# A decoder of four layers on one core: half of each layer norm's normalising moves from ScalarE to GpSimd, and the order tables are laid anew

## The reference

```python
def _layernorm(x, axis=-1, eps=1e-05):
    m = jnp.mean(x, axis=axis, keepdims=True)
    v = jnp.var(x, axis=axis, keepdims=True)
    return (x - m) / jnp.sqrt(v + eps)
```

## Time and profile before

| | us |
|---|---|
| median of 3 runs | 5380.19 |
| lowest and highest | 5375.60, 5387.07 |
| span of the profiled execution | 5378.0 |
| PE busy | 4667.4 (87%) |
| DVE busy | 3288.8 (61%) |
| ACT busy | 2478.0 (46%) |
| POOL busy | 779.1 (14%) |

### The profile page before, as it was taken

The page is one execution under the profiler, slowest core; times in us unless marked ns, Lnnn a source line. Parts: engine busy times, 40 slices in busy tenths (PEclk is TensorE's granted clock), DMA queues, the critical chain, the costliest instruction groups (busy, mean ns, idle before and its releaser), DMA issues.

```text
span 5378.0 us, 128488 instructions
## 1 busy us (share of the span) xinstructions
PE 4667.4 (87%) x54601; PEld 3416.4 (64%) x54601; DVE 3288.8 (61%) x8433; ACT 2478.0 (46%) x5054; POOL 779.1 (14%) x841
## 2 busy tenths in 40 slices
PE   5668878899898989889898989889898989898877
PEld 4346656677676767666676767666676767666554
DVE  6754677555657475656657575656757575756542
ACT  3325545435444454444545454444545454544331
POOL 5550100101011110101011110101011111101000
PEclk7678989999899999999999999999999999999997
DMA  1132100012110101111010101111010101010000
GB/s 63 28 98 64 33 2 2 4 52 61 33 32 11 58 17 47 28 39 36 15 51 11 54 20 47 28 39 36 21 44 11 54 20 50 24 35 25 11 22 28
DMA packets 154184, 181.62 MB, mean 34 GB/s; under 512 B 62890, under 2 KB 82450, under 8 KB 152850
## 3 DMA queue, kind: packets, MB, share of 16 engines
q1 hardware_dynamic: 153618, 173.41, 10.8%
HBM read 162.50 MB, written 10.55 MB: 32 GB/s over the span
## 4 chain that ended last, share of the span: by engine, by line
PE 64%; DVE 16%; ACT 7%; issue 5%; POOL 1%; DMA 0%; SPq 0%; POOLq 0%; DVEq 0%; ACTq 0%
PE g_pair L2759 8%; PE g_pair L2774 8%; PE g_pair L1626 6%; DVE g_tops L1703 6%; PE g_pair L1599 6%; PE g_pair L1649 5%; ACT g_keys_exps L1679 4%; PE g_pair L1996 2%; PE g_pair L1986 2%; PE g_pair L1433 1%; PE g_pair L1611 1%; PE g_pair L1660 1%; PE g_pair L2060 1%; PE g_pair L2360 1%; PE g_pair L1569 1%
## 5 line engine op out<-in xcount | busy, mean ns | idle before, releaser
L1679 ACT ACTIVATE g_keys_exps<-g_pair 128x1024 f32<-128x1024 f32 (+1 forms) x768 | 745.8, 1018 | 646.9 <-PE g_pair L1626 645.8
L1703 DVE TENSOR_REDUCE g_tops<-g_pair 128x8 f32<-128x1024 f32 (+1 forms) x768 | 748.7, 1006 | 329.8 <-PE g_pair L1599 328.1
L1412 POOL TENSOR_TENSOR g_rstd<-g_rstd,minus_half 128x4 f32<-128x4 f32 x224 | 231.2, 1033 | 3578.1 <-DVE g_rstd L1394 3573.5
L2774 PEld LDWEIGHTS g_pair<-region,g_keys_exps 128*128 128x128 f32 x4096 | 514.1, 192 | 142.6 <-issue 133.0
L2759 PE MATMUL g_pair<-g_xT,region 128*128 128x512 f32 x1024 | 551.9, 621 | 9.6 <-DVE g_keys_exps L2799 4.4
L2774 PE MATMUL g_pair<-region,g_keys_exps 128*128 128x128 f32 x4096 | 546.1, 278 | 4.5 <-DVE g_base L2806 3.9
L1626 PE MATMUL g_pair<-g_qa,g_keys_exps 32*77 32x128 f32 (+1 forms) x12288 | 463.5, 290 | 72.8 <-DVE g_o L1724 46.5
L1649 PE MATMUL g_pair<-g_keys_exps,g_v 77*32 77x128 f32 (+1 forms) x12288 | 444.9, 289 | 83.7 <-DVE g_tops L1703 74.7
L1626 PEld LDWEIGHTS g_pair<-g_qa,g_keys_exps 32*77 32x77 f32 (+1 forms) x12288 | 397.8, 175 | 171.7 <-DVE g_o L1724 78.8
L1599 PE MATMUL g_pair<-g_keys_exps,g_qa 32*128 32x256 f32 (+1 forms) x6144 | 392.5, 371 | 101.5 <-ACT g_keys_exps L1679 84.1
L1649 PEld LDWEIGHTS g_pair<-g_keys_exps,g_v 77*32 77x32 f32 (+1 forms) x12288 | 333.7, 115 | 200.3 <-DVE g_tops L1703 140.0
(11 more groups left out here) (379 smaller groups left out, 8541.9 us busy)
## 6 DMA issues: line engine op xcount, KB each, us to landing
region<-L_w_in SPq DMA_DIRECT2D x512, 256.0 KB, 2.9
region<-xT_in SPq DMA_DIRECT2D x16, 256.0 KB, 2.8
z_scratch<-m_z SPq DMA_DIRECT2D x4, 1024.0 KB, 5.4
g_qa<-xT_in SPq DMA_DIRECT2D x16, 256.0 KB, 2.9
g_oT_sc<-z_scratch SPq DMA_DIRECT2D x64, 64.0 KB, 2.6
g_o<-x_in SPq DMA_DIRECT2D x16, 256.0 KB, 3.1
out<-g_x SPq DMA_DIRECT2D x16, 256.0 KB, 2.3
setup_weights<-prepared_in SPq DMA_DIRECT2D x1, 2589.5 KB, 10.7
```

The source lines that it names most:

```text
L1412: e.tensor_tensor(g.rstd[:, :], g.rstd[:, :], g.s["minus_half"], ALU.pow).then_inc(*b.gpsimd(st + " rstd"))
L1679: e.activation(g.p[0:nk, 2 * k:2 * k + 2, :, :].rearrange("p g u q -> p (g u q)"), b.pair[st][k][0:nk, :, :].rearrange("p r c -> p (r c)") ...
L1703: e.tensor_reduce(top_columns(g, k), src, AX, ALU.max).then_inc(*b.vector(f"{st} top {n} {k}"))
L2774: ins = e.matmul(bank[1][:, n * D:(n + 1) * D], g.gated_hid[:, x % 2, c, n * T:(n + 1) * T], weights.part(f"w2 {x}", c), start=c == n == 0 ...
```

## The change

ACT's two operations of each norm go (`normalize_scalar` is deleted, 448 operations over the kernel). `normalize_gpsimd` takes them over, behind its power, in the form DVE uses: (x - mean) x rstd with two per-partition scalars, as a TENSOR_SCALAR on POOL, each waiting for the power's result. Since that form needs no shift, DVE's shift operation goes too (224). All who waited for ACT's "normal 2" or "normal 3" now wait for POOL's. `ORDER` of all five engines and `GIVEN` are laid anew; the opening's tables stay as they are. The steps of a batch number 291 on PE as before, 190 on ACT (218 before), 474 on DVE (488) and 61 on POOL (33).

```diff
     yield from between
-    e.wait_ge(*b.gpsimd[st + " rstd"])
-    e.scalar_tensor_tensor(out=g.shift[:, :], in0=g.mean_var[:, :, 0], scalar=-1.0, in1=g.rstd[:, :],
-                           op0=ALU.mult, op1=ALU.mult).then_inc(*b.vector(st + " shift"))
-    yield
     for n in range(2):
         e.wait_ge(*b.gpsimd[st + " rstd"])
         e.tensor_scalar(out[:, n, :], src[:, n, :], g.mean_var[:, n, 0:1], g.rstd[:, n:n + 1],
...
-def normalize_gpsimd(e, b, st):
+def normalize_gpsimd(e, b, st, src, out):
 
     g = b.g
     e.wait_ge(*b.vector[st + " variance"])
     e.tensor_tensor(g.rstd[:, :], g.rstd[:, :], g.s["minus_half"], ALU.pow).then_inc(*b.gpsimd(st + " rstd"))
     yield
-
-
-def normalize_scalar(e, b, st, src, out):
-
-    g = b.g
-    e.wait_ge(*b.vector[st + " shift"])
     for n in range(2, SEQS):
-        e.activation(out[:, n, :], src[:, n, :], ACT.Identity, bias=g.shift[:, n:n + 1], scale=g.rstd[:, n:n + 1]
-                     ).then_inc(*b.scalar(f"{st} normal {n}"))
+        e.wait_ge(*b.gpsimd[st + " rstd"])
+        e.tensor_scalar(out[:, n, :], src[:, n, :], g.mean_var[:, n, 0:1], g.rstd[:, n:n + 1],
+                        ALU.subtract, ALU.mult).then_inc(*b.gpsimd(f"{st} normal {n}"))
         yield
...
-            e.wait_ge(*b.scalar[f"{st} normal {n}"])
+            e.wait_ge(*b.gpsimd[f"{st} normal {n}"])
...
-    yield from normalize_scalar(e, b, st, g.x, g.x)
     e.wait_ge(*b.tensor[st + " turned"])
...
-    e.wait_ge(*b.scalar["end normal 3"])
+    e.wait_ge(*b.gpsimd["end normal 3"])
```

The first row of PE's table, before and after (one digit a step):

```diff
-        "00001101200201021002000021010000122020000001001012121121121112212111121221201012011200000002100001002202"
+        "00101010202010210201020000010001022020000100110010112121211121221211121222101021012002100022000200100001"
...
```

More of the change, by code:

```diff
@@ L432 @@
[L432 to L438 removed]
+        "01000020000011110200222101002122000011011122111222111021002201000200000100012120101112111101100102110000"
@@ L488 @@
     "scalar": (
[12 rows of a table removed]
[L501 removed]
[5 rows of a table removed]
[10 rows of a table added]
+        "f2 first probs 0|f2 exp 1|f2 first probs 1|f2 exp 2|f2 first probs 2|f2 exp 3|f2 first probs 3|f2 combined|"
[4 rows of a table added]
         "f3 hid 4|f3 hid 6|f3 hid 8|f3 hid 10|f3 hid 12|f3 hid 14|f3 hid 16|f3 hid 18|f3 hid 20|f3 hid 22|f3 hid 24|"
[L508 removed]
[1 row of a table added]
     "vector": (
         "rec v|rec weights|rec sum|rec stats 0|rec stats 1|rec stats 2|rec stats 3|rec moments 0|rec moments 1|"
[21 rows of a table removed]
[20 rows of a table added]
         "a2 v first|a2 v|a2 top 0 0|a2 top 0 1|a2 q shifted 0|a2 top 1 0|a2 top 1 1|a2 q shifted 1|a2 top 2 0|"
@@ L1462, in base_gpsimd @@
     e.wait_ge(*b.vector[before + " normal 1"])
-    e.wait_ge(*b.scalar[before + " normal 3"])
+    e.wait_ge(*b.gpsimd[before + " normal 3"])
     e.tensor_tensor(g.base[:, :, :], g.x[:, :, :], over(g.r[row], 1, SEQS), ALU.add).then_inc(*b.gpsimd(st + " base"))
@@ L1849, in recurrent_gpsimd @@
     yield
-    yield from normalize_gpsimd(e, b, "rec")
+    yield from normalize_gpsimd(e, b, "rec", b.g.x, b.g.x)
 def raw_context_tensor(e, b):
@@ L2689, in conv_scalar @@
     yield from project_out_scalar(e, b, "f3")
-    yield from normalize_scalar(e, b, "f3 mid", g.o, g.base)
     e.wait_ge(*b.tensor["f3 mid turned"])
@@ L2734, in conv_gpsimd @@
     yield
-    yield from normalize_gpsimd(e, b, "f3 mid")
+    yield from normalize_gpsimd(e, b, "f3 mid", g.o, g.base)
     e.wait_ge(*b.tensor["f3 mid turned"])
@@ L2816, in end_vector @@
     yield from normalize_vector(e, b, "f3 out", g.base, g.o)
-    e.wait_ge(*b.scalar["f3 out normal 3"])
+    e.wait_ge(*b.gpsimd["f3 out normal 3"])
     e.wait_ge(*b.vector["f3 out normal 1"])
@@ L2918, in first_half_gpsimd @@
             yield from latent_gpsimd(e, b)
-        yield from normalize_gpsimd(e, b, st)
+        yield from normalize_gpsimd(e, b, st, b.g.x, b.g.x)
 def second_half_tensor(e, b):
@@ L2952, in second_half_scalar @@
     yield from gated_scalar(e, b)
-    yield from normalize_scalar(e, b, "f3 out", g.base, g.o)
-    yield from normalize_scalar(e, b, "end", g.x, g.x)
 def second_half_vector(e, b):
@@ L2978, in second_half_gpsimd @@
     yield from base_gpsimd(e, b, "x2", "a2", "x2_bo")
-    yield from normalize_gpsimd(e, b, "x2")
-    yield from normalize_gpsimd(e, b, "f2")
+    yield from normalize_gpsimd(e, b, "x2", b.g.x, b.g.x)
+    yield from normalize_gpsimd(e, b, "f2", b.g.x, b.g.x)
     yield from rotary_gpsimd(e, b)
     yield from base_gpsimd(e, b, "a3", "f2", "a3_bo")
-    yield from normalize_gpsimd(e, b, "a3")
-    yield from normalize_gpsimd(e, b, "x3")
+    yield from normalize_gpsimd(e, b, "a3", b.g.x, b.g.x)
+    yield from normalize_gpsimd(e, b, "x3", b.g.x, b.g.x)
     yield from conv_gpsimd(e, b)
-    yield from normalize_gpsimd(e, b, "f3 out")
-    yield from normalize_gpsimd(e, b, "end")
+    yield from normalize_gpsimd(e, b, "f3 out", b.g.base, b.g.o)
+    yield from normalize_gpsimd(e, b, "end", b.g.x, b.g.x)
 def loads_sync(e, b, dram, first):
```

367 lines of the change are left out of this document (181 added, 186 removed), and 120 rows, old and new, of the table BATCH.

## The result

The change makes the kernel 3.1% faster: 5214.32 us median of 4 runs (5209.52 to 5216.58) beside 5378.28 for the kernel before on the same chip, a ratio of 0.9694 with a 95% interval of 0.9676 to 0.9712. The prediction had 5362 us and a range down to 5294.

The account below looks back on a forecast made before the run. PE was taken as busiest, with 524 us of its idle time all that the change could affect. Terms -16 + 4 + 12 + 0 - 18 = -18 us gave 5362 us; the range of 8 in 10 was 5294 to 5426.

Parts of the forecast that it names:

- T: Length of POOL's new 128x128 normalising TENSOR_SCALAR: taken as 0.5 us, with 0.22 and 1.24 as the ends.
- Part 1: ScalarE loses 448 normalising operations, so PE's 194 us of waits for ACT shrink: -16 us.
- Part 2: VectorE loses 224 shift operations but collides with POOL's new operation at the shared port: net +4 us.
- rule of shares: PE's waits for an engine change by the same share as that engine's load.
- Part 3: Each norm takes 0.27 us longer, from power to last normalising, stretching 43 waits at transposes: +12 us.
- the slope: Change of the forecast sum with the length of POOL's new operation: some 110 us for each us.
- Rival A: Slower: VectorE stands still at the port while POOL normalises, and PE gets it in full; 5406 us, chance 0.19.
- Part 4: POOL's longer queue, and SP's store and table now mixing batches' loads among the weights': 0 us.
- Part 5: Relaid tables of all engines and PSUM pairs mix PE's steps more finely: -18 us, bounds -75 and +30.
- Rival C: The tables bring much: idle time falls with same-batch neighbours, -75 us instead of -18; 5305 us, chance 0.16.

Follow-up runs that it names:

- the move alone: The changed code run in the old order, with the tables and pairs of the kernel before: 5380.56 us, ratio 1.0025 to the kernel before.
- the tables alone: The code of the kernel before, ScalarE still normalising, run in the changed kernel's new order: 5233.31 us, ratio 0.9746 to the kernel before.
- the mixed one: The kernel before with 180 swaps in PE's table, x x y y into x y x y, other tables unchanged: 5447.22 us, ratio 1.0135.

## Why the prediction missed the size

**T.** Forecast 0.5 us, measured 0.83 in the mean, between the ends but above the span of 0.4 to 0.65 in which the forecast was to hold. The fills of POOL were the wrong neighbours. The nearest in kind was the TENSOR_SCALAR of 308 elements at 1238 ns. Scaled by elements alone it gives 0.51 us; what that leaves out is the part that is there for a single column, 411 ns in the run with one column. The Trainium skill's page "GPSIMD Engine Reference", section 3.1, gives 2.6 cycles an element for two inputs, which makes an estimate of 0.28 us plus dispatch. The runs disagree: 833 ns, and between the two lengths measured (833 - 411)/127 = 3.3 ns for each further element, about 4 cycles at that page's 1.2 GHz instead of its 2.6.

**Part 1, ScalarE's relief (-16).** ACT's busy time fell by 166 us, and PE's waits for it from 194 to 148, below the 180 foreseen. But in the move alone, where nothing else is relaid, ACT is 177 us less busy and these waits are 178 us. That is the 16 us of the sum in size, though some 6 of it were transposes that now wait for POOL instead, so about 10 are relief.

**Part 2, the collisions (+4).** The step of this part that failed is that VectorE would be held by POOL's new operation. It isn't: 346 ns (median) beside 341, a mean of 375 where 0.6 us was forecast. Counted from the trace, 373 of VectorE's 448 normalising operations overlap in time with L1409 of POOL. Only 14 of the 448 take over 500 ns, and each of these 14 overlaps a 128x512 TENSOR_TENSOR of POOL; none is long beside L1409 alone. The two collisions that I had read the earlier trace rows were real, but in each POOL ran a TENSOR_TENSOR; I carried them over to an operation with one SBUF tile on each side. The Trainium skill's page "SBUF — State Buffer", section "Who interferes with whom", calls the shared pair of ports an exclusive lock, and makes no exception for POOL's one-tile operation; the trace of after doesn't show that lock here. With hardly any collisions VectorE is 44.5 us less busy in the move alone (3288.8 to 3244.3), by the rule of shares 4 us *gained*.

**Part 3, latency (+12).** T was wrong, the norm's own length was right: with T = 0.83, "0.08 + 2T" is 1.74 us, which is what the last norm shows. At 12 us per 0.27 the 0.63 more would cost 28. What isn't borne out is that the transposes pay it: their waits went from 38 to 47 us in the move alone, 9 us.

**The move in all.** -16 - 4 + 28 = +8, measured +13 (7 to 20). With T and the missing lock put right, the sum of the first three parts gives the move in the old order, and the slope is near too, 105 for 110. Both agreements are in part luck, because the terms don't stand where the prediction put them. In the move alone PE's waits changed by -16 for ACT, +9 for VectorE and +19 for POOL, where the corrected terms want -16, -4 and +28. With POOL's operation cut to one column the transposes wait 22 us instead of 30, less than a fifth of the 44 us gained. Where the rest of the latency's price is paid isn't settled. Rival A's mechanism didn't happen: VectorE isn't held by L1409. Its sign is that of the move alone.

**Part 4 (0).** Right on POOL's queue, with 4% of the chain instead of 1% and 15 us of PE's waits. Wrong on SP: that its table mixes the loads was seen and set at nothing, and it costs about 35 us.

**Part 5, the tables (-18, bounds -75 and +30).** This is the term that makes the miss: alone the tables bring some 137 us, almost twice the bound. Rival C named the right term, with half its size and a reason that fell. Three things were wrong. The count was: 1528 and 1301 of 4656 stood for 1644 and 1395 of 5040. The cause was: mixing more finely costs 1.35%. And the step that failed in the sum was to let the tables act on idle time alone, "the matmuls themselves stay". In the kernel with the tables alone PE's idle time fell by 74.6 us, which is the bound of -75 (by luck, since the count it came from is no measure), and its busy time fell by 60.3 us, for which the sum has no term at all. In the changed kernel it is 90 and 80. PE's groups of before, then of after (busy us, mean ns):

```profile
L2759 PE MATMUL g_pair<-g_xT,region 128*128 128x512 f32 x1024 | 551.9, 621 | 9.6 <-DVE g_keys_exps L2799 4.4 <-ACT g_keys_exps L2787 3.1
...
L1626 PE MATMUL g_pair<-g_qa,g_keys_exps 32*77 32x128 f32 (+1 forms) x12288 | 463.5, 290 | 72.8 <-DVE g_o L1724 46.5 <-DVE g_qa L1706 21.1 <-ACT g_oT_sc L1673 3.9
L1649 PE MATMUL g_pair<-g_keys_exps,g_v 77*32 77x128 f32 (+1 forms) x12288 | 444.9, 289 | 83.7 <-DVE g_tops L1703 74.7 <-ACT g_keys_exps L1679 7.6
```

```profile
L2745 PE MATMUL g_pair<-g_xT,region 128*128 128x512 f32 x1024 | 546.3, 615 | 8.1 <-ACT g_keys_exps L2773 4.1
...
L1636 PE MATMUL g_pair<-g_keys_exps,g_v 77*32 77x128 f32 (+1 forms) x12288 | 434.8, 285 | 69.9 <-DVE g_tops L1690 62.1
L1613 PE MATMUL g_pair<-g_qa,g_keys_exps 32*77 32x128 f32 (+1 forms) x12288 | 449.9, 284 | 42.8 <-DVE g_o L1711 28.9
```

The three lose 5.6, 10.1 and 13.6 us, with as many instructions of the same shapes. For the two of attention the traces show what happened. A matmul of L1626 takes 277 ns in the mean where the granted clock is 2.4 GHz and 422 where it is 1.2; after the change (L1613) it is 276 and 420. What moved is how many run at the lower level, 1149 before and 682 after. L1649 goes the same way (276 and 418 ns both times, 1172 and then 760 at the lower level). Over all matmuls, split by group and level, 39 of the 80 us come from fewer of them at the lower level. The remaining 41 or so are less busy time within a level, 20 of them in the 128x512 matmuls that read `g_xT`, L2759 among them; their cause is open. In the table above, kernels with more idle time have, by and large, more busy time too (the mixed one is an exception, with 54 us more idle and 8 less busy than before, and 27 us less at 1.2 GHz). So the clock is a part of the gain, and it also disturbs small comparisons: 13 executions of the kernel before on one chip run from 5355 us at a mean clock of 0.939 to 5380 us at 0.933. By this column an order that makes PE wait less mostly also keeps it longer at 2.4 GHz; no run changes one without the other. Part of such a difference may be how the profile books a short wait inside a step, since the ends of matmuls are modelled; the span, at any rate, has it in full.

**What stays open.** Which engine's table, or the order of the PSUM pairs, carries the 2.5% isn't settled. The tables name one common order of steps, and exchanging PE's, or those of VectorE, ScalarE and POOL, one side at a time would make the engines wait for each other in a circle (worked out from the waits in the code, not run); only SP's could be put back, from the new to the old. What distinguishes the good order is open too. Neither the count of neighbours nor the order of readiness is it. What the traces show is that the gain is spread evenly: from the start of one batch to the next it is about 302 us before and 291 after, and a batch is in flight for 898 and 868 us (counted from the traces). PE's waits became fewer in nearly every stage, not in one, by the same count.

## What to carry to other kernels

Where several streams are interleaved by written tables, an edit that relays them is to be costed by the tables first: here they moved the time by 2.5%, and the operation that the edit was about by 0.25% one way or 0.5% the other. A count read off a table is no measure of it, and the bound for an unmeasured order should be as wide as what orders have been seen to do, not a share of today's idle time: busy time moves with it. When two kernels differ by half a per cent, compare the granted clock of their executions before giving the difference a cause. For an operation whose duration no row has, take the row that is nearest in kind (engine and instruction), not the one nearest in size, and test a collision with the very pair of instructions that will meet.

## What the runs showed of the hardware

- POOL's TENSOR_SCALAR of 128x128 with two per-partition scalars takes 0.80 us (median); with one column it takes 0.38 us.
- It does not hold VectorE's TENSOR_SCALAR on the same kind of tile: 346 ns beside 341, with 373 of 448 overlapping. POOL's TENSOR_TENSORs of 128x512 did (1.23 us; all 14 of over 500 ns after the change).
- PE's busy time is not fixed by its instructions. The same 54601 matmuls took from 4555 to 4745 us in these kernels, depending on the order of work around them. About half of the 80 us by which the change shortened it are matmuls that no longer ran at 1.2 GHz: one of L1626 takes 422 ns there and 277 at 2.4 GHz.
- In this kernel 125 exchanges of neighbouring steps among the 5040 of PE's table cost 3.3 points.
